# Flamingo gated block: in the GELU slots the first exponentials go ahead of the second ones on ScalarE, and one group of transposed scores moves behind the next slot's scores on TensorE

## What is computed

```python
q = layernorm(x) @ Wq.T + bq ; k, v = ctx @ Wk.T + bk, ctx @ Wv.T + bv     # per head
qk = q @ k.T ; scores = qk / 4
feats = [mean(scores), mean(max(scores)), mean(var(softmax(scores)))]       # per batch and head
t = exp(clip(w3 @ gelu(w2 @ gelu(w1 @ feats + b1) + b2) + b3))
attn = softmax(qk / (2 t)) ; x = x + tanh(g) * ((attn @ v) @ Wo.T + bo)
x = x + tanh(g2) * quantised_ffn(layernorm(x))                              # 28 tiles of 128 rows
```

## Time and profile before

| | |
|---|---|
| time before | median 792.87 us of 3 runs (788.21 to 796.98) |
| profiled execution | 792.8 us, span of its instructions 791.0 us, mean granted TensorE clock 0.962 |
| busy | PE 702.7 us, DVE 708.0, ACT 683.9, GpSimd 487.9 |
| the attention pipeline | about 25 to 690 us of the span |
| one pair of rows (16 slots) in its steady part | 38.0 us |

### The profile page before, as it was taken

One profiled execution on the slowest core, in us unless ns is written; L12 is line 12 of the kernel. 1 busy time (PEld: TensorE's weight loads), 2 busy tenths in 40 slices (PEclk: granted clock), 3 DMA queues, 4 the chain that ended last, 5 costly groups with the idle time before them and its releaser, 6 DMA issues.

```text
span 791.0 us, 20866 instructions
## 1 busy us (share of the span) xinstructions
PE 702.7 (89%) x7118; PEld 474.6 (60%) x7127; DVE 708.0 (90%) x1452; ACT 683.9 (86%) x1454; POOL 487.9 (62%) x956
## 2 busy tenths in 40 slices
PE   6567899999999999999999999999999888877896
PEld 4334566666666666667676766676765555533453
DVE  5779899989899999999999999899999776798995
ACT  1578899898999999999999999999999888768883
POOL 4747657667777667676766666767664043245663
PEclk9666899999999999999999999999999899999998
DMA  9997747464668575767455666656664122246688
GB/s 206 204 261 166 197 127 149 109 126 128 154 120 149 124 144 124 145 122 158 123 138 134 134 137 133 128 136 130 124 118 85 39 68 86 71 103 164 160 179 181
DMA packets 148887, 108.50 MB, mean 137 GB/s; under 512 B 56991, under 2 KB 145183, under 8 KB 148767
## 3 DMA queue, kind: packets, MB, share of 16 engines
q1 hardware_dynamic: 143630, 101.98, 58.3%
q10 hardware_dynamic: 5152, 5.19, 2.7%
HBM read 49.54 MB, written 12.85 MB: 79 GB/s over the span
## 4 chain that ended last, share of the span: by engine, by line
PE 36%; ACT 35%; DVE 16%; issue 9%; DMA 2%; ACTq 1%; POOL 1%; SPq 0%; DVEq 0%; POOLq 0%
ACT ex L1197 13%; ACT pt L1187 12%; PE p_o L1348 7%; PE p_m L1426 6%; PE p_s L1328 5%; PE p_m L1407 5%; PE p_t L1369 4%; DVE kst L1032 3%; DVE hmax L1035 3%; PE p_m L1415 3%; ACT L1223 3%; ACT L1187 2%; DVE stats L907 2%; PE p_m L1399 2%; DVE nm L926 2%
## 5 line engine op out<-in xcount | busy, mean ns | idle before, releaser
L1197 ACT ACTIVATE ex<-p_s,nm 112x375 f32<-112x375 f32 x512 | 275.8, 618 | 12.3 <-DVE nm L926 11.0
L1187 ACT ACTIVATE pt<-p_t,ct 128x336 f32<-128x336 f32 x488 | 245.8, 577 | 26.7 <-PE p_t L1369 24.5
L907 DVE BATCH_NORM_STATS2 stats<-ex 112x6 f32<-112x375 f32 x512 | 252.5, 535 | 1.4 <-ACT ex L1197 1.3
L926 DVE TENSOR_REDUCE nm<-p_s 112x2 f32<-112x750 f32 x256 | 236.0, 922 | 1.2 <-PE p_s L1328 1.0
L1328 PE MATMUL p_s<-kst,qst 96*112 96x375 bf16 x512 | 154.8, 348 | 13.5 <-ACT ex L1197 7.3
L1369 PE MATMUL p_t<-qst,kst 99*128 99x112 bf16 x1464 | 115.1, 213 | 4.9 <-ACT pt L1187 4.0
L1369 PEld LDWEIGHTS p_t<-qst,kst 99*128 99x128 bf16 x1464 | 91.1, 98 | 44.0 <-issue 19.7
L1407 PE MATMUL p_m<-wv_sb,ctxt 128*128 128x256 f32 (+1 forms) x384 | 106.7, 401 | 4.7 <-DVE va L859 2.9
L1348 PE MATMUL p_o<-pt,va 128*32 128x112 f32 (+1 forms) x3072 | 101.7, 265 | 1.4 <-ACT pt L1187 0.8
L1426 PE MATMUL p_m<-ctxt,wk_sb 128*128 128x375 f32 x240 | 94.6, 518 | 1.7 <-DVE qf L875 1.1
L1328 PEld LDWEIGHTS p_s<-kst,qst 96*112 96x112 bf16 x512 | 67.0, 139 | 45.7 <-ACT ex L1197 34.6
(11 more groups left out here) (187 smaller groups left out, 1164.3 us busy)
## 6 DMA issues: line engine op xcount, KB each, us to landing
kst<-kp SPq DMA_DIRECT2D x378, 93.8 KB, 3.5
ctxt<-ctxt_dram SPq DMA_DIRECT2D x32, 375.0 KB, 4.2
qbounce<-qp SPq DMA_DIRECT2D x32, 168.0 KB, 2.5
qst<-qbounce SPq DMA_DIRECT2D x32, 168.0 KB, 3.6
qst<-qbounce SPq DMA_DIRECT2D x32, 112.0 KB, 3.4
xm<-x_dram SPq DMA_DIRECT2D x32, 112.0 KB, 2.4
x_dram<-x SPq DMA_DIRECT2D x32, 112.0 KB, 1.9
xt<-x_dram SPq DMA_DIRECT2D x28, 128.0 KB, 3.2
```

What stands on the lines that cost most here:

```text
L907: last = nc.vector.bn_stats(stats[:, nb % RING, 2 * pb + i], ex[0:SQ, 2 * (t % 2) + i, :])
L926: nc.vector.tensor_reduce(nm[:, n % RING, 2 * p:2 * p + 2], p_s[t % 2][0:SQ, :, 0:SK], axis=AX.X, op=ALU.max, negate=True).then_inc(s_max, 1)
L1187: nc.scalar.activation(pt[:, (2 * r + i) % 8], st_home(r, i)[:, 0:KC * SQ].rearrange("k (c q) -> k c q", c=KC), ACT.Exp, scale=ct[:, nr % ...
L1197: nc.scalar.activation(ex[0:SQ, 2 * ((t - 1) % 2) + i, :], p_s[(t - 1) % 2][0:SQ, i, 0:SK], ACT.Exp, bias=nm[:, ne % RING, h:h + 1]).then_ ...
```

## The change

In ACT's GELU slot and the three slots behind it (`firsts_lead`) the first exponentials stand ahead of the second ones. On PE the transposed scores of the GELU slot (`scores_late`) are left out there and done in the next slot, right behind its scores. This is so for the GELU slots of rows 4 to 30, 14 in all; in row 2 no second exponentials exist yet, and row 32 is left out by the condition.

```diff
--- before.py
+++ after.py
@@ -345,6 +345,17 @@
         def pair_of(n):
 
             return n % 2 == 0 and 2 <= n <= B
+
+
+        def scores_late(t):
+
+            n, p = divmod(t, SLOTS)
+            return p == SLOTS - 1 and pair_of(n) and t + 1 < SLOTS * B
+
+
+        def firsts_lead(t):
+
+            return any(scores_late(t - back) for back in range(4))
 
 
         def roomy_row(n):
@@ -1171,31 +1182,41 @@
                     if m > 0:
                         act.wait_ge(s_ob, count(1, m))
                     nc.scalar.copy(oa[:, :, :], o_acc).then_inc(s_oc, 1)
-                r = t - BACK - 1
-                if 0 <= r < SLOTS * B:
-
-                    nr, pr = divmod(r, SLOTS)
-                    if r % 2 == 0 and r >= 4:
-                        act.wait_ge(s_pv, count(4, nr, pr // 2 - 1))
-                    for i in range(2):
-                        h = 2 * pr + i
-                        act.wait_ge(s_st, count(2 * SLOTS, nr, h + 1))
-                        if h == 0 and nr % 2 == 0:
-                            act.wait_ge(s_c, nr // 2 + 1)
-                        if r == 0 and i == 0:
-                            act.wait_ge(s_raw, 5)
-                        nc.scalar.activation(pt[:, (2 * r + i) % 8], st_home(r, i)[:, 0:KC * SQ].rearrange("k (c q) -> k c q", c=KC), ACT.Exp,
-                                             scale=ct[:, nr % RING, h:h + 1]).then_inc(s_e2, 1)
-                if 0 <= t - 1 < SLOTS * B:
-
-                    ne, pe_ = divmod(t - 1, SLOTS)
-                    act.wait_ge(s_max, count(SLOTS, ne, pe_ + 1))
-                    if t - 1 >= 2:
-                        act.wait_ge(s_bn, count(SLOTS, ne, pe_ - 1))
-                    for i in range(2):
-                        h = 2 * pe_ + i
-                        nc.scalar.activation(ex[0:SQ, 2 * ((t - 1) % 2) + i, :], p_s[(t - 1) % 2][0:SQ, i, 0:SK], ACT.Exp,
-                                             bias=nm[:, ne % RING, h:h + 1]).then_inc(s_e1, 1)
+                def second():
+
+                    r = t - BACK - 1
+                    if 0 <= r < SLOTS * B:
+
+                        nr, pr = divmod(r, SLOTS)
+                        if r % 2 == 0 and r >= 4:
+                            act.wait_ge(s_pv, count(4, nr, pr // 2 - 1))
+                        for i in range(2):
+                            h = 2 * pr + i
+                            act.wait_ge(s_st, count(2 * SLOTS, nr, h + 1))
+                            if h == 0 and nr % 2 == 0:
+                                act.wait_ge(s_c, nr // 2 + 1)
+                            if r == 0 and i == 0:
+                                act.wait_ge(s_raw, 5)
+                            nc.scalar.activation(pt[:, (2 * r + i) % 8], st_home(r, i)[:, 0:KC * SQ].rearrange("k (c q) -> k c q", c=KC), ACT.Exp,
+                                                 scale=ct[:, nr % RING, h:h + 1]).then_inc(s_e2, 1)
+                def first():
+
+                    if 0 <= t - 1 < SLOTS * B:
+
+                        ne, pe_ = divmod(t - 1, SLOTS)
+                        act.wait_ge(s_max, count(SLOTS, ne, pe_ + 1))
+                        if t - 1 >= 2:
+                            act.wait_ge(s_bn, count(SLOTS, ne, pe_ - 1))
+                        for i in range(2):
+                            h = 2 * pe_ + i
+                            nc.scalar.activation(ex[0:SQ, 2 * ((t - 1) % 2) + i, :], p_s[(t - 1) % 2][0:SQ, i, 0:SK], ACT.Exp,
+                                                 bias=nm[:, ne % RING, h:h + 1]).then_inc(s_e1, 1)
+                if firsts_lead(t):
+                    first()
+                    second()
+                else:
+                    second()
+                    first()
                 if copying and 0 < t < BACK:
                     copy_k()
                 for i in (1, 2, 0):
@@ -1349,7 +1370,7 @@
                                       start=(c == 0), stop=(c == KC - 1))
                     last.then_inc(s_pv, 1)
 
-                def scores_t():
+                def scores_t(r):
 
                     nr, pr = divmod(r, SLOTS)
                     if pr == 0:
@@ -1371,7 +1392,9 @@
 
                 weighted = 0 <= g < SLOTS * B and g % 2 == 1
                 if 0 <= r < SLOTS * B and t >= TAIL:
-                    scores_t()
+                    scores_t(r)
+                if 0 < r and scores_late(t - 1):
+                    scores_t(r - 1)
                 if p == 1 and pair_of(n - 1):
                     pe.wait_ge(s_lt, (n - 1) // 2)
                 if p == 3 and 0 <= n - 1 < B:
@@ -1459,8 +1482,8 @@
                     pe.wait_ge(s_g2, n // 2)
                     mm(t_h3, w3b[:, :], hid2[:, :], start=True, stop=True).then_inc(s_h3, 1)
 
-                if 0 <= r < SLOTS * B and t < TAIL:
-                    scores_t()
+                if 0 <= r < SLOTS * B and t < TAIL and not scores_late(t):
+                    scores_t(r)
 
                 if t == TOT_AT:
                     pe.wait_ge(s_abs, 6)
```

## The result

The changed kernel took 798.45 us (median of 20 runs, 795.51 to 801.63) against 795.48 (20 runs, 788.21 to 798.61), a ratio (of the means, 798.69 and 793.93) of **1.006 with a 95% interval of 1.0035 to 1.0085**: slower by 4.8 us by the means, by 3.0 us by the medians. The forecast was 4.2 us slower, a ratio of 1.0053.

A forecast was written before the change was run, and what follows sets the result against it. ACT was taken to bound each pair from the GELU network to 329, PE afterwards; no saving and 0.30 us a pair added, 14 times, 4.2 us on 792.8, gave 797.0 us, range 795.6 to 798.4.

The forecast's parts named there:

- What bounds: Whole pair of rows: ACT sets the period from the GELU network to 329, PE afterwards; ACT's lateness is handed on whole.
- No saving: ACT's exchange and PE's scores of T+1 starting 0.30 us earlier save zero; DVE's idle of 1.19 stays.
- Steps 1 and 2: ACT reaches `ct` at 318.20 as before; PE's transposed scores of T+1 wait for later second exponentials, PE some 0.3 late.
- Steps 3 to 5: T+2 to T+6: K projection 0.31 us late, T+3's first exponentials wait 0.11, `pv` and second K copy 0.35 late.
- step 5: PE in T+3: `pv` 0.35 us late, passed through output projection, `x` and second K projection to ACT in T+6.
- step 3: PE in T+2 and T+3: K projection 0.31 us late, so ACT stands still about 0.25 before the `kf` copy.
- Step 6: From T+4 ACT is gapless again; shorter records give back up to 0.10, so the period grows 0.25 to 0.35 us.
- The sum: Over 14 pairs: 3.5 to 4.9 us, taken as 4.2 at 0.30 a pair; 792.8 becomes 797.0 us.
- No change: Late K projections in T+3 and T+6 are covered by existing waits: 792.8 us; chance 0.20.
- Faster: Scores bound DVE's maxima of T+1, so earlier scores gain 4.9 us: 788; chance 0.10.
- Much slower: The K projection and `pv` delays add up instead of overlapping, 0.60 us a pair: 801.2, 802 and more; chance 0.13.
- The clock: New PE stops behind the GELU slot drop the clock to 1.2 GHz for one slot, 34 us: 827; chance 0.02.

The follow-up runs named there:

- late_0_2: Changed kernel with the transposed scores of T+2 also moved behind the next slot's scores, besides those of T; 796.64 us (1 run), period 38.36 us.
- lead11: Kernel before with first exponentials leading only in place 2 of the even rows (T+11), row 2 left as it was; 794.95 us (1 run), period 38.04 us.
- lead6: Kernel before with first exponentials leading only in the slot ahead of the GELU slot (T-1); 790.50 us (12 runs), ratio 0.9949, period 37.77 us.
- lead9: Kernel before with first exponentials leading only in place 0 of the even rows (T+9), row 2 left as it was; 790.94 us (1 run), period 37.87 us.
- act_only: Changed kernel with the GELU slot's transposed scores left in that slot, ACT's new order kept; 800.60 us (1 run), period 38.54 us.
- late4: Changed kernel with the transposed scores of T to T+3, not T alone, moved behind the next slot's scores; 795.06 us (10 runs), ratio 1.0018.
- lead2: Changed kernel with first exponentials leading in two slots (T, T+1) in place of four; 797.05 us (1 run), period 38.27 us.
- pe_only: Changed kernel with ACT's old order restored, only PE's transposed scores of the GELU slot moved; 800.48 us (1 run), period 38.60 us.
- lead6_9: Kernel before with first exponentials leading in places 6 and 0 of the even rows (T-1, T+9); 787.40 us (7 runs), ratio 0.9909.

## Why the prediction was right

- *What bounds.* That ACT sets the period from the GELU network to the exponentials of 327.96, and PE behind them, held for the change: what ACT was late there, 0.30, the period grew by. late_0_2 and lead11 fit the same division. lead6 and lead9 show that it was too simple elsewhere: PE's part held a wait for ACT (the scores of T+10, 0.68 long in place of 0.48), and ahead of the GELU network ACT's own order was worth 0.27.
- *No saving.* Right: the maxima of T+1 didn't move (315.23 against 315.22) though the scores came earlier, and the idle of 1.19 stayed. act_only shows what that move is good for all the same: without it the maxima are late, and the price is 0.50. The wait of the exponentials' table load, which the prediction took as nothing, was nothing: it starts 2.27 behind the GELU load in both kernels (314.99 and 311.44).
- *Steps 1 and 2.* The transposed scores of T+1 wait as forecast. Their second head was to be issued by 316.78; six matmuls that start at 316.24 and last 0.76 end at 317.00, which is the same forecast plus the length of one such matmul (0.21 on average).
- *Steps 3 to 5.* K projection forecast 319.08, measured 319.16; first K copy 320.56 and 320.62; first exponentials of T+3 318.65 and 318.65; `pv` 321.17 and 321.17; second K copy 325.16 and 325.15. With both waits gone (late4) 0.1 is left; with the first alone shortened by 0.09 (late_0_2) nothing is gained. So step 5's delay is the binding one, and step 3's is included in it, as step 5 said, but it binds by little: by the starts ACT stops for 0.10 ahead of the exponentials of T+3, 0.20 ahead of the first K copy and 0.03 ahead of the second, so most of the 0.34 by which the second copy is late is there at the first. The sign that the prediction gave, idle time in front of `kf` with PE's K projection named, did not show: the profile names none in this stretch, as stops of this size vanish under the overlap of the records.
- *Step 6.* The exponentials at 328.32 start 0.36 late and end 0.30 late: 0.06 came back, not 0.10. They lasted 1.12, and I had let them be as short as 1.07. That puts the growth at 0.30, in the middle of 0.25 to 0.35.
- *The sum.* 14 x 0.30 = 4.2 us on 792.8; the medians differ by 3.0 us, the ratio gives 4.8 us (2.8 to 6.8). Nearer than this the total time can't tell; the period and the 4.28 us over 13 pairs can. That the time came within 1.5 us of the 797.0 forecast says less: over 20 runs the kernel before had a median of 795.48, 2.6 us above the one of three runs that the forecast started from.
- *The rivals.* No change: the late projections are not covered. Faster: DVE came to the scores by its own work. Much slower: the two delays overlap.
- *The clock.* It stayed at 1.00 in the steady part in spite of the new stops of up to 0.27 us on PE. That it would was less certain than the prediction's reading of one window, as late4 shows in another pair: its PE had the same 1.12 of idle there as in every GELU slot, and this time the granted clock fell to 0.50, its 1.2 GHz level, just behind it (timeline and window of late4):

```profile
277.22 0.30 PE L1416 MATMUL p_o<-hid,w2t_sb 64*64 64x32 f32 x2 [1.12 <-ACT hid L1247]
...
280.00:282.00 2.00, 2.00 (x6) 1.12 (x6) 0.13 (x1) 1.05 (x3) 0.38 (x2) 0.50 1.04 150
```

That pair took 39.69 us in place of 38.16. lead2 had one such pair as well, of 39.63 in place of 38.27; the other steady pairs of both kernels had the same stop and stayed at 1.00. So one fall costs 1.4 to 1.5 us, not the 2.4 of the prediction. The Trainium skill, "TensorE: Matmul & The Clock Gate", section "HAM oscillation - how this bites in real kernels", ties the fall to waits for DMA that are longer than these stops. By that alone the prediction's word that the change is a danger was too strong, and in late4 and lead2 the trace has falls behind a shorter stop.

## What to carry to other kernels

When two producers on one engine serve two consumers, as the two kinds of exponentials on ACT do here, exchanging them gained nothing where that engine never idled; it only made one consumer late, and what stood behind that consumer in its stream was late too. The exchange paid at another place: where the engine stood still for the first of the two while the input of the second was ready, and where nothing behind the stop brought the wait back (lead6 and lead9 against lead11). Halves of a change can each be worse than the whole, so test them both before one of them is blamed; and if the steady part of a trace repeats to 0.02 us, its period decides questions that the total time, with its 0.5% of scatter, leaves open.

## What the runs showed of the hardware

- **A stop can be larger than the idle time that the profile names.** On ACT the record of one instruction reaches over the start of the next. The stop ahead of the second exponentials in lead6's place showed as 0.12 and was 0.31 by the starts, and removing it gained 0.27. The stop of 0.2 in lead2 showed as no idle row at all. Starts should be subtracted, not gaps read.
- **How far a record reaches over grows while ACT runs without a stop.** A pair of first exponentials lasts 1.04 behind the table load and 1.18 after 14 us of gapless work, while the next instruction starts 0.91 to 0.94 behind it in both, and it is back at 1.04 behind the stop of 0.80 at 331.74. It also fell from 1.12 to 1.07 across `ct` and `nmt`, where no stop shows. A consumer on another engine is released at the end of the record, so after a stop it gets its data up to 0.14 us sooner relative to the start.
- **The steady periods of a kernel agree within 0.02 us**; the pairs of 39.69 in late4 and 39.63 in lead2, with a mean granted clock of 0.96, were the exceptions. Beginning and end of a run, where the mean granted clock was 0.73 to 1.00, differ by 1 to 3 us from run to run.
- **A stop of 1.12 us on PE can be followed by a fall of the granted clock to 0.50, or not.** The same stop stands in the GELU slot of every steady pair; the fall came behind it in one pair each of late4 and lead2 and in none of the kernel before and the change. In six traces (act_only, pe_only, late4, lead6, lead9 and lead6_9) the pair ahead of the steady ones had a mean of 0.96 too, without that stop just ahead of the fall. What decides it isn't shown.
